# A reordered front and a first expert layer split into three fp32r products

## The reference

```python
df = -(grad(A0*f, 1) + grad(A1*f, 2)) + 0.5*(grad2(B0*f, 1) + grad2(B1*f, 2) + 2 cross differences of B2*f)
x = maximum(f + df * dt, 0)
h = layernorm(x) * ln_g + ln_b                  # over the 128 features
h = (h - mean(h, tokens)) * rsqrt(var(h, tokens) + 1e-8)
gamma, beta = split(mlp(subj_emb[ids]))         # a small net of four layers on 8 ids
h = h * (softplus(gamma) + 1e-8) + beta
probs = softmax(h @ router_w); gates = top2(probs), normalised
hid = relu(h @ exp_w1[e] + exp_b1[e])           # 8 experts, 128 -> 512
y = sum over e of gate[e] * (hid @ exp_w2[e] + exp_b2[e])
out = x + y
```

## Time and profile before

| what | value |
|---|---|
| runs | 118.13, 118.04 and 117.0 us, median 118.04 |
| profiled execution | 117.75 us, of which the span from first to last instruction is 115.9 us |
| PE busy | 110.3 us (95% of the span) |
| DVE, ACT, POOL busy | 90.9, 78.6, 8.1 us (78%, 68%, 7%) |
| chain that ended last | PE 83%, DVE 6%, DMA 5% |
| granted TensorE clock | 1.000 over the span |

### The profile page before, as it was taken

The page is one execution under the profiler, slowest core; times in us unless marked ns, Lnnn a source line. Parts: engine busy times, 40 slices in busy tenths (PEclk is TensorE's granted clock), DMA queues, the critical chain, the costliest instruction groups (busy, mean ns, idle before and its releaser), DMA issues.

```text
span 115.9 us, 1542 instructions
## 1 busy us (share of the span) xinstructions
PE 110.3 (95%) x509; PEld 85.5 (74%) x509; DVE 90.9 (78%) x202; ACT 78.6 (68%) x110; POOL 8.1 (7%) x16
## 2 busy tenths in 40 slices
PE   6989999999999999999999999999999999999970
PEld 2679686357546788888888888888888888888860
DVE  0549889789990796999959967996799589879781
ACT  0934647775634997777777777777777777777900
POOL 3421740000000000000000000000000000000040
PEclk9999999999999999999999999999999999999999
DMA  3999991000000550120400230040005000400004
GB/s 85 308 357 411 424 403 73 0 0 3 0 0 11 150 212 6 62 119 0 181 0 0 79 105 0 0 155 31 0 0 181 0 0 0 187 0 0 0 0 181
DMA packets 4439, 10.79 MB, mean 93 GB/s; under 512 B 784, under 2 KB 1744, under 8 KB 4432
## 3 DMA queue, kind: packets, MB, share of 16 engines
q1 hardware_dynamic: 3776, 9.66, 22.7%
q10 hardware_dynamic: 656, 1.04, 2.8%
HBM read 10.15 MB, written 0.56 MB: 92 GB/s over the span
## 4 chain that ended last, share of the span: by engine, by line
PE 83%; DVE 6%; DMA 5%; issue 1%; SPq 1%; ACT 1%; DVEq 0%; ACTq 0%
PE zt L700 11%; PE zt L702 11%; PE zt L701 11%; PE yt L694 6%; PE aux L728 6%; PE aux L724 6%; PE aux L725 6%; PE zt L678 5%; PE yt L728 5%; PE yt L724 5%; PE yt L725 5%; DMA gt<-in_grids_exchanged_dram 5%; PE yt L670 1%; SPq L309 1%; PE zt L577 1%
## 5 line engine op out<-in xcount | busy, mean ns | idle before, releaser
L528 ACT ACTIVATE hid_hi<-zt,pv 128x1024 fp32r<-128x1024 f32 x27 | 30.2, 1120 | 17.4 <-PE zt L702 17.2
L1042 DVE TENSOR_TENSOR hid_lo<-hid,hid_hi 128x1024 fp32r<-128x1024 f32 x27 | 33.0, 1221 | 10.0 <-issue 5.5
L533 ACT ACTIVATE hid<-zt,pv 128x1024 f32<-128x1024 f32 x27 | 29.9, 1109 | 0.0
L700 PE MATMUL zt<-h_hi,ws 128*128 128x512 f32 x56 | 22.7, 406 | 0.0
L701 PE MATMUL zt<-h_hi,ws 128*128 128x512 f32 x56 | 21.8, 390 | 0.0
L702 PE MATMUL zt<-h_lo,ws 128*128 128x512 f32 x56 | 21.8, 389 | 0.0
L700 PEld LDWEIGHTS zt<-h_hi,ws 128*128 128x128 f32 x56 | 10.5, 188 | 2.9 <-issue 0.5
L701 PEld LDWEIGHTS zt<-h_hi,ws 128*128 128x128 f32 x56 | 10.5, 188 | 2.5 <-issue 0.5
L702 PEld LDWEIGHTS zt<-h_lo,ws 128*128 128x128 f32 x56 | 10.5, 188 | 2.2
L725 PE MATMUL aux<-hid_hi,ws 128*128 128x512 f32 (+1 forms) x32 | 12.0, 376 | 0.0
L728 PE MATMUL aux<-hid_lo,ws 128*128 128x512 f32 (+1 forms) x32 | 12.0, 376 | 0.0
(11 more groups left out here) (149 smaller groups left out, 146.3 us busy)
## 6 DMA issues: line engine op xcount, KB each, us to landing
we<-in_exp_w_dram SPq DMA_DIRECT2D x8, 512.0 KB, 9.4
gate_all<-gates_dram SPq DMA_DIRECT2D x8, 512.0 KB, 3.6
f<-in_x_dram SPq DMA_DIRECT2D x2, 256.0 KB, 4.9
ft<-in_x_exchanged_dram ACTq DMA_DIRECT2D x2, 256.0 KB, 6.0
out_dram<-acc SPq DMA_DIRECT2D x2, 128.0 KB, 1.9
out_dram<-acc ACTq DMA_DIRECT2D x1, 256.0 KB, 2.1
first<-d_difference_dt_ids_dram ACTq DMA_DIRECT2D x1, 136.0 KB, 3.5
gn<-in_grids_dram SPq DMA_DIRECT2D x1, 128.0 KB, 3.7
```

The lines of the kernel that those rows point to most:

```text
L528: act.activation(hid_hi[:, c, :], zt[c % 2][:], ACT.Relu, bias=bias).then_inc(hi_ready, 1)
L533: act.activation(hid[:, c, :], zt[c % 2][:], ACT.Relu, bias=bias).then_inc(hid_ready, 1)
L700: pe.matmul(zt[c % 2][:, tok], w_hi, h_hi[:, tok], start=True, stop=False)
L1042: v.tensor_tensor(hid_lo[:, c, :], hid[:, c, :], hid_hi[:, c, :].bitcast(F32), ALU.subtract).then_inc(lo_ready, 1)
```

## The change

- **Loads.** `gt` goes from SP's queue to ACT's (third there), p64 from ACT's queue to `gt`'s place on SP's.
- **The small net.** Its tiles become full 128x128: DVE fills rows 64 to 127 of `pw`, its last 64 columns and half of `sty1` with zeros at the start, PE waits for these (`zeros_ready`), and `HW2` and `SW1` change places in p128, so that the wide slice of `SW1` stays inside.
- **Warm-up.** Eight matmuls in place of seven, on a constant tile of ones; the tile `warm` and the wait for it go.
- **Order.** DVE makes `u_a1` of half 1 ahead of `s_b2`; POOL waits for `s_b2`. PE issues two of half 0's four `wT` matmuls behind net layer 2, two of half 1's `wT` matmuls ahead of `norm_transposed(0)`, and `step_transposed(0)` ahead of `second_rows_b`. ACT makes `hyp2` between two pairs of ReLUs, and copies `acc` of half 0 ahead of its share of `h`.
- **Expert 0, layer 1, half 1.** Its four fp32 matmuls become twelve fp32r matmuls on new tiles `w0_hi` (ACT, a copy, L495 of the new file) and `w0_lo` (POOL, a subtraction, behind half 0's first two tiles of `h`). PE runs both halves of the router's logits ahead of it, and waits for `w0_hi`, `w0_lo` and half 1's `h_hi` and `h_lo`. DVE makes the parts of half 1 first, then those of half 0.

The diff, cut:

```diff
-WARM_START = 7
+WARM_START = 8
...
 RW_AT = 6
-HW2_AT = RW_AT + E
-SW1_AT = HW2_AT + SH
-BIAS_AT = SW1_AT + SE
+SW1_AT = RW_AT + E
+HW2_AT = SW1_AT + SE
+BIAS_AT = HW2_AT + SH
 NB = C + 1
...
+        w0_hi = sb("w0_hi", [P, C, P], F32R, align=512)
+        w0_lo = sb("w0_lo", [P, C, P], F32R, align=512)
...
+        w0_hi_ready = sem("w0_hi_ready")
+        w0_lo_ready = sem("w0_lo_ready")
...
-            load(gt[:], gridsT, gt_in)
+            load(pw[0:SE, 0:N64], p64, p64_in)
...
-            pool.wait_ge(a1_ready[1], 1)
+            pool.wait_ge(s_ready[1], 1)
...
+            pool.wait_ge(w0_hi_ready, 1)
+            pool.wait_ge(h_ready, H_DVE[0])
+            pool.tensor_tensor(w0_lo[:], we[:, 0, 0], w0_hi[:].bitcast(F32), ALU.subtract).then_inc(w0_lo_ready, 1)
...
             act.dma_start(first[:], first_operands).then_inc(first_in, 16)
-            act.dma_start(pw[:], p64).then_inc(p64_in, 16)
             act.dma_start(ft[:, 0:BH, :], xT[:, 0:BH, :]).then_inc(ft_in[0], 16)
+            act.dma_start(gt[:], gridsT).then_inc(gt_in, 16)
             act.dma_start(ft[:, BH:B, :], xT[:, BH:B, :]).then_inc(ft_in[1], 16)
             act.preload_act_table_set("natural_log_exp_and_others")
...
-            def first_half_relu():
-
-                for b in range(BH):
-                    act.wait_ge(step_ready, b // 2 + 1)
+            def first_half_relu(k):
+
+                act.wait_ge(step_ready, k + 1)
+                for b in range(2 * k, 2 * k + 2):
                     act.activation(xs[:, b, :], own(b), ACT.Relu).then_inc(xs_ready, 1)
...
+            def first_weights_high():
+
+                act.wait_ge(w_in[0], 16)
+                act.activation(w0_hi[:], we[:, 0, 0], ACT.Copy).then_inc(w0_hi_ready, 1)
...
-            first_half_relu()
+            first_half_relu(0)
             hyper_second()
+            first_half_relu(1)
             style_first()
             inverse_sd_features(0)
             style_parts()
             style_log()
             normalise(0)
             style_shift()
+            first_weights_high()
             inverse_sd_tokens(0)
+            transposed_step(0)
             conditioned(0)
-            transposed_step(0)
             second_half_relu(0, 2)
...
-                    pe.matmul(warm_ps.rearrange("p (k j) -> p k j", k=BH), warm[:], over_batches(warm[:]), start=True, stop=True)
-
-            def net_layer(n, weights, acts, rows):
+                    pe.matmul(warm_ps, ones(P), ones(HT), start=True, stop=True)
+
+            def net_layer(n, weights, acts):
                 if n > 0:
                     pe.wait_ge(net_sb, n)
-                pe.matmul(small[0:rows, 0:B], weights, acts, start=True, stop=True).then_inc(net_ps, 1)
...
-            def first_columns_w():
+            def first_columns_w(k):
...
-                for k in range(2):
-                    for b in of_pair(0, k):
-                        last = pe.matmul(own(b), wT[:, b, :], dt_diff[:, b, :], start=False, stop=True,
-                                         skip_group_check=True)
-                    last.then_inc(step_ready, 1)
+                for b in of_pair(0, k):
+                    last = pe.matmul(own(b), wT[:, b, :], dt_diff[:, b, :], start=False, stop=True, skip_group_check=True)
+                last.then_inc(step_ready, 1)
...
-            def second_columns_w():
+            def second_columns_w(k):
 
                 pe.wait_ge(w_op_ready, 2)
-                for b in range(BH, B):
+                for b in of_pair(1, k):
                     pe.matmul(own(b), wT[:, b, :], neg_diff, start=False, stop=False, skip_group_check=True)
...
-                if n == 1:
+                if n == 0:
+                    pe.matmul(z0[c], we[:, 0, 0, c, :], h[:, half(0)], start=True, stop=True).then_inc(z0_ready, 1)
+                else:
                     pe.wait_ge(hid0_ready, c + 1)
-                pe.matmul(z0[c], we[:, 0, 0, c, :], h[:, half(n)], start=True, stop=True).then_inc(z0_ready, 1)
+                    pe.matmul(z0[c], w0_hi[:, c, :], h_hi[:, half(1)], start=True, stop=False)
+                    pe.matmul(z0[c], w0_lo[:, c, :], h_hi[:, half(1)], start=False, stop=False)
+                    pe.matmul(z0[c], w0_hi[:, c, :], h_lo[:, half(1)], start=False, stop=True).then_inc(z0_ready, 1)
...
-            pe.wait_ge(warm_ready, 1)
             keep_warm(WARM_START)
...
-            net_layer(0, pw[0:NS, EMB_AT:EMB_AT + SE], onehot[:], SE)
+            pe.wait_ge(zeros_ready, 3)
+            net_layer(0, pw[:, EMB_AT:EMB_AT + P], onehot[:])
             first_columns_b()
-            net_layer(1, pw[:, HW1_AT:HW1_AT + SH], se[:], SH)
-            first_columns_w()
+            net_layer(1, pw[:, HW1_AT:HW1_AT + SH], se[:])
+            first_columns_w(0)
             pe.wait_ge(p128_in, 16)
-            net_layer(2, pv[:, HW2_AT:HW2_AT + SH], hyp1[:], SH)
+            net_layer(2, pv[:, HW2_AT:HW2_AT + SH], hyp1[:])
+            first_columns_w(1)
             step_cross(1, 0)
-            net_layer(3, pv[:, SW1_AT:SW1_AT + SE], hyp2[:], SE)
+            net_layer(3, pv[:, SW1_AT:SW1_AT + P], hyp2[:])
             step_cross(1, 1)
             pe.wait_ge(net_sb, 4)
             pe.matmul(small[:, 0:B], pw[:, SW2_AT:SW2_AT + P], sty1[:], start=True, stop=True)
             pe.matmul(small[:, B:2 * B], pw[:, SW2_AT + P:SW2_AT + 2 * P], sty1[:], start=True,
                       stop=True).then_inc(net_ps, 1)
             second_rows_a()
+            second_columns_w(0)
             pe.wait_ge(ident_ready, 1)
             pe.wait_ge(xs_ready, BH)
             norm_transposed(0)
-            second_columns_w()
+            second_columns_w(1)
             second_columns_b()
+            step_transposed(0)
             second_rows_b()
-            step_transposed(0)
...
             pe.wait_ge(h_ready, sum(H_DVE))
             pe.wait_ge(h_act_ready, B - sum(H_DVE))
-            layer1_0(1, 0)
             logits(1)
-            for c in range(1, C):
+            pe.wait_ge(w0_hi_ready, 1)
+            pe.wait_ge(w0_lo_ready, 1)
+            pe.wait_ge(h_hi_ready, 1)
+            pe.wait_ge(h_lo_ready, 1)
+            for c in range(C):
                 if c == C - 1:
                     pe.wait_ge(acc_ready, HALVES)
                 layer1_0(1, c)
             pe.wait_ge(ld_ready, 1)
             for c in range(C - 1):
                 layer2_0(1, c)
-            pe.wait_ge(h_hi_ready, 1)
-            pe.wait_ge(h_lo_ready, 1)
+            pe.wait_ge(h_hi_ready, HALVES)
+            pe.wait_ge(h_lo_ready, HALVES)
             layer1(1, 0)
...
-            v.memset(warm[:], 0.0).then_inc(warm_ready, 1)
+            v.memset(pw[SE:P, :], 0.0).then_inc(zeros_ready, 1)
+            v.memset(pw[0:SE, N64:NPW], 0.0).then_inc(zeros_ready, 1)
+            v.memset(sty1[SE:P, :], 0.0).then_inc(zeros_ready, 1)
...
-            def input_parts():
-
-                v.wait_ge(h_ready, sum(H_DVE))
-                v.wait_ge(h_act_ready, B - sum(H_DVE))
-                v.tensor_copy(h_hi[:], h[:]).then_inc(h_hi_ready, 1)
-                v.wait_ge(h_hi_ready, 1)
-                v.tensor_tensor(h_lo[:], h[:], h_hi[:].bitcast(F32), ALU.subtract).then_inc(h_lo_ready, 1)
+            def input_parts(n, made):
+
+                tok = half(n)
+                v.wait_ge(h_ready, sum(H_DVE[:n + 1]))
+                v.wait_ge(h_act_ready, (n + 1) * BH - sum(H_DVE[:n + 1]))
+                v.tensor_copy(h_hi[:, tok], h[:, tok]).then_inc(h_hi_ready, 1)
+                v.wait_ge(h_hi_ready, made)
+                v.tensor_tensor(h_lo[:, tok], h[:, tok], h_hi[:, tok].bitcast(F32), ALU.subtract).then_inc(h_lo_ready, 1)
...
+            v.wait_ge(ft_in[1], 16)
+            product(u_a1, ft, 1, a1_grid).then_inc(a1_ready[1], 1)
             v.wait_ge(f_in[1], 16)
             product(s_b2, f, 1, b2_grid).then_inc(s_ready[1], 1)
-            v.wait_ge(ft_in[1], 16)
-            product(u_a1, ft, 1, a1_grid).then_inc(a1_ready[1], 1)
...
-            input_parts()
+            input_parts(1, 1)
+            input_parts(0, HALVES)
...
-         given["router_w"], given["hyp_w2"], given["sty_w1"], expert_biases], axis=1)
+         given["router_w"], given["sty_w1"], given["hyp_w2"], expert_biases], axis=1)
```

More of the change, by code:

```diff
@@ L52 @@
 N64 = EMB_AT + SE
+NPW = EMB_AT + P
 def constants():
@@ L93, in build @@
         pv = sb("pv", [P, N128])
-        pw = sb("pw", [SE, N64])
+        pw = sb("pw", [P, NPW])
         we = sb("we", [P, E, 2, C, P], align=512)
-        warm = sb("warm", [P, P], mybir.dt.bfloat16)
         s_b2 = sb("s_b2", [P, B, P])
@@ L137, in build @@
         h_lo = sb("h_lo", [P, T], F32R, align=512)
[L139 to L145, removed]
+        w0_hi = sb("w0_hi", [P, C, P], F32R, align=512)
+        w0_lo = sb("w0_lo", [P, C, P], F32R, align=512)
+        idf = sb("idf", [P, B])
+        idn = sb("idn", [P, B])
+        idw = sb("idw", [P, B])
+        idc = sb("idc", [P, B])
```

(21 more changed lines are left out.)

## The result

The changed kernel takes 117.00 us (median of 17 runs) beside 117.87 of the kernel before on the same chip: ratio 0.9926, interval 0.9907 to 0.9946, so 0.87 us less, with 0.64 to 1.10 inside the interval. One of the 17, 119.08, is a slow run and stays out of the ratio. The forecast was 0.94 less.

The account below looks back on a forecast made before the run. It took the chain from the load `gt` to `h`, then PE's matmuls, to bound the kernel. Front 0.25, `acc` copy 0.07 and split 0.62 sum to 0.94 us off 117.75: forecast 116.8, range 115.9 to 117.7.

Parts of the forecast that it names:

- The front: Chain from the load `gt` to ACT's `h` of half 0: 0.25 us sooner, with `h` moving along.
- the split: Expert 0, layer 1, half 1 as twelve fp32r products: stretch 4.60 us in place of 5.22, 0.62 less.
- the copy to `acc`: ACT's copy of half 0 moved ahead of `h`: gain 0.07 us, bounds 0 and 0.15.
- The loads: `gt`, third on ACT's queue, lands at 7.43 in place of 7.68: 0.25 us sooner, bounds 0 and 0.37.
- The first rival: Front gives more: `sq` not held by POOL, `gt` comes by its issue; 0.2 and 0.12 more, 116.5 us, chance 0.25.
- `sq` held: DVE's `sq` ends only with POOL's second product, so at 13.77 less 0.25, however early PE delivers.
- what PE and ACT do sooner: Reordered PE and ACT work between 9 and 13 us: gain eaten by POOL's end, put at 0, other bound 0.2.
- The eighth warm-up matmul: Opening on PE: pushes PE back by 0.46 us at most, showing on the side that waits for POOL: 0.
- Cost 0: DVE's opening zero fills come while DVE has nothing to do, so they cost 0.
- The loads give nothing: Rival: `gt` lands at 7.68 as before, since the bytes ahead come over the same engines; 117.06 us, chance 0.15.
- slower: Rival: p64 lands late and PE waits for it at net layer 0; 118.2 us if at 9.75, chance 0.05.

Follow-up runs that it names:

- split alone: Kernel before with only the three fp32r products of expert 0's layer 1, half 1, their parts and order, no new front: 117.21 us, ratio 0.9954.
- two fills less: New kernel with two of DVE's six opening fills made by GpSimd: 116.75 us, ratio 0.9933.
- before, two fills more: Kernel before with two small opening fills of an unread tile added to DVE's stream: 118.33 us beside 117.73, ratio 1.0035.
- front alone: New kernel with expert 0's layer 1 for half 1 back in fp32 as before: 117.28 us, ratio 0.9969.
- late weights: New kernel with the weights of experts 3 to 7 loaded only when half 0 is normalised: 116.80 us, ratio 0.9908.
- two fills more: New kernel with two more small fills, of a tile nobody reads, at the start of DVE's stream: one execution, 117.61 us.
- low part later: New kernel, but PE waits for `h_lo` only ahead of the third product, the first that reads it: 116.67 us, ratio 0.9914.
- both mended: New kernel with two opening fills on GpSimd and PE's wait for `h_lo` only ahead of the third product: 116.54 us, ratio 0.9899.
- both, late weights: New kernel with two fills on GpSimd, the later `h_lo` wait, and weights of experts 3 to 7 held back: 116.67 us, ratio 0.9914.

## Why the prediction was right, and where its steps were not

The total came out as forecast, 0.87 beside 0.94, but of three terms that were wrong in size and one that was missing. The front gave more up to `sq` than was priced, the split and the copy to `acc` less, and a pause took a part back; that these errors offset each other is luck.

**The loads: mis-sized, and past the bound.** The step "it landed at 7.43: 0.25 us sooner" took the landing of what had stood third on ACT's queue; its bound, 0.37, was the difference of the issues. `gt` landed 1.23 sooner in the two profiles. One load is not to be judged by the slot ahead of it alone: with the queues changed, this one took 4.8 from issue to landing beside 5.6, and over the ten runs with the new loads it took 4.2 to 5.5 (landing at 5.9 to 7.2), over the four with the old ones 4.5 to 5.6 (6.6 to 7.7). Landing times scatter by a us from run to run; the price taken from one of them had no more precision than that. The first rival ("the front gives more") was the one to look at, and its bound was too near as well.

**`sq` held: right as a mechanism, gone in the result.** The prediction kept the hold because it had `gt` only 0.25 sooner. The runs show both sides: with the loads put back, and with GpSimd's product held back, `sq` lasts until that product ends; in the new kernel GpSimd is over 0.78 ahead of it. The Trainium skill (SBUF — State Buffer, "SBUF: two separate sides") has the port pair of DVE and GpSimd as an exclusive lock kept for a whole instruction; the 0.66 and the 0.45 agree. So what PE and ACT do sooner, which I put at 0, counted after all.

**How much the front gained.** The end of `sq` cannot be compared from one profile each. PE's four opening transposes of `f` took 1.03 to 2.04 us in these runs, with the old order as with the new. On the timeline of the split alone:

```profile
4.00 2.04 PE L599 MATMUL yt<-f,ident 128*128 128x256 f32 x4
```

and on that of the kernel with two fills less:

```profile
3.99 1.03 PE L606 MATMUL yt<-f,ident 128*128 128x256 f32 x4
```

One by one, the second to the fourth start 0.43 us apart in the first case (4.56, 4.98, 5.41) and 0.21 in the second (4.20, 4.42, 4.63). The profile gives a granted clock of 1.00 for the windows of both, but the trace has no record of the clock there: its first record, of full clock, begins at 6.45 in the first and at 3.83 in the second. In all fourteen runs the matmuls of the opening lie 0.43 apart ahead of that moment and 0.21 behind it (the narrower ones behind the transposes 0.21 and 0.11). So PE opens at the lower of its two levels (1.2 and 2.4 GHz), the warm-up included, whose 512 columns take 0.43 where those of a later product take 0.23, and it rises at 3.58 to 6.70, with matmuls running since 0.76 (0.97 in the old order). What sets that moment stays open. The table has it as "full clock from":

| kernel | full clock from | transposes, us | `sq` ends |
|---|---|---|---|
| before | 4.25 | 1.23 | 13.77 |
| split alone | 6.45 | 2.04 | 14.15 |
| before, two fills more | 6.55 | 1.97 | 14.14 |
| new kernel | 5.51 | 1.59 | 13.42 |
| front alone | 5.38 | 1.62 | 13.25 |
| late weights | 4.31 | 1.12 | 12.79 |
| `acc` behind `h` | 3.58 | 1.10 | 12.91 |
| two fills more | 6.70 | 1.91 | 13.72 |
| low part later | 5.45 | 1.62 | 13.32 |
| two fills less | 3.83 | 1.03 | 13.13 |
| both mended | 4.40 | 1.17 | 13.67 |
| both, late weights | 3.79 | 1.03 | 13.01 |

The two runs in which GpSimd holds `sq` (the loads put back, GpSimd's product over `sq`) are left out. At an early rise the new front is 0.76 to 0.98 ahead (13.01, 12.91 and 12.79 beside 13.77, of the one profile of the kernel before), at a late one 0.43 (13.72 beside 14.15); the two kernels with 13.13 and 13.67 are those in which DVE waited 1.05 and 1.37 for `gn`, a load that the change does not touch. At a late rise the chains of the old order begin with the warm-up, and not with `gt`, and GpSimd is over (12.72 and 13.74) before `sq` starts (14.00 and 13.98): there the gain is not that of the loads but of the rest of the new front, which I had put at 0. That the front begins with `gt` was true of the profile that I had, and not of every execution.

The profiled run of the new kernel rose later than that of before, and `f` landed 0.56 later (4.38, where the earlier trace rows gives 3.1 from the issue at 0.72), so that PE's products behind the transposes began at 5.94 in place of 5.05; that is why it shows 0.35. The eighth warm-up matmul, put at 0 too, is not free either: in six of the ten kernels with the new loads the chain begins with the warm-up, which in five of them ends at 4.33, where the seven of the split alone end at 4.14.

By the prediction's own measure ("I am wrong if the front gains half a us or more") the step was wrong up to `sq` at an early rise. Up to `h`, behind the pause, the front alone gave 0.37 by its time, with the half us inside the interval.

**The pause: missing.** It takes 0.25 to 0.28 back behind `sq`, in each of the nine kernels with six or more opening fills on DVE, whatever the loads, the weights or ACT's order. It stands ahead of the 62nd instruction that the kernel writes for DVE, waits on semaphores that stand alone counted: `shift` in the new kernel, `scale` with two fills more, `shift` in the kernel before with two fills more. With two fills fewer, and in the kernel before, that instruction is the second `h` of DVE, and no pause shows there: `xp` behind it starts 0.64 or 0.65 after the first `h`, as in the new kernel (18.14 to 18.78). That the first `h` covers it is likely, and not shown. My line "Cost 0" for DVE's zeros looked at their time alone. That place and pause go together is shown; what DVE does there is not. The Trainium skill (Runtime: NRT & Kernel Launch, "Instruction fetch mechanics") says that an engine fetches its instructions ahead, in blocks of 256, and that the cost is mostly hidden. That does not explain the pause: here the place is the 62nd, the cost is not hidden, and in the front alone the trace has no packet of instructions between the start of the span and the end of the pause.

**The copy to `acc`: 0.07 forecast, 0 measured.** It lay within its bounds.

**The split: mis-sized.** 0.62 forecast, 0.33 in the profile, 0.31 to 0.38 over the chains of all kernels that have it with this wait. Products at 0.23, weights' parts hidden, DVE's order: all as said. The wait is the whole difference. From the start of the logits the first product was to start after 1.76 (1.62 and 0.14) and started after 2.07. The cast took 0.43 where I had halved 0.69 to 0.36, the low part came 0.08 late for that and for its start, and PE started 0.30 behind the end of the low part where I had 0.07, for which the prediction names no row. By the chain PE was through the logits only at 28.64, so it stood for 0.22 with the low part finished. With that wait taken off the path the stretch took 4.53, near the 4.46 that the prediction summed without a wait.

**The other rivals.** p64 landed at 8.00 and not by 7.68, but PE reached net layer 0 only at 8.62: no wait. "The loads give nothing" and "slower" had no part.

Together, as an estimate from these single profiles: 0.76 to 0.98 of the front, less 0.25, and 0.33 of the split make 0.84 to 1.06 with an early rise, and with a late one (0.43) 0.51; the 0.87 of the medians lies among them.

## What to carry to other kernels

Price a load that moves by several executions, since its landing scatters by more than the slot is worth; see whether the chain begins with it in each of them, and ask what the front becomes if it comes a whole us sooner. When small instructions are added at the head of an engine's stream, look for a pause "issue" of 0.25 that was not there, and move it, by a fill or two on another engine, to a place with cover. A wait for several operands is best put ahead of the first instruction that reads each of them: here that was worth as much as the split itself.

## What was not expected of the hardware

- A pause of 0.25 us ahead of a fixed place in DVE's stream (the 62nd instruction of this kernel's), moved at will by two fills more or fewer; 0.4 us (0.05 to 0.78) on the old kernel.
- The same four opening transposes on PE take 1.03 to 2.04 us from run to run. The profile reads a granted clock of 1.00 there, but the trace's record of full clock begins only at 3.58 to 6.70, and ahead of it the matmuls lie twice as far apart (0.43 and 0.21).
- PE started 0.30 us after the end of the last operand on DVE (0.26 with the split alone) when it had waited for it together with three others; with this wait two products later it had no gap at all.
- An operation on 128x4 elements of DVE took 0.45 and 0.66 in place of 0.15 under a product of GpSimd, to the end of that product within 0.01.
